# A rotary-embedding product moved from GpSimd to VectorE in a one-core attention and expert block

## The reference

```
q = x @ Wq.T + bq ; k = x @ Wk.T + bk ; v = x @ Wv.T + bv      # 16 heads of 64
def _rotate_half(x):
    half = x.shape[-1] // 2
    return concatenate([-x[..., half:], x[..., :half]], -1)
q = q * cos + _rotate_half(q) * sin
k = k * cos + _rotate_half(k) * sin
attn = softmax(einsum('bhqd,bhkd->bhqk', q, k) * scale)
out  = einsum('bhqk,bhkd->bhqd', attn, v)
x = layernorm(x + out @ Wo.T + bo)
x = layernorm(x + experts(x))
```

## Time and profile before

| | |
|---|---|
| median of 3 runs | 249.88 us (248.84 to 250.79) |
| the profiled execution | 248.74 us |
| its span, first to last instruction | 246.9 us |
| VectorE busy | 189.5 us (77%) |
| TensorE matmuls busy | 186.0 us (75%) |
| ScalarE busy | 157.4 us (64%) |
| GpSimd busy | 146.1 us (59%) |
| mean granted TensorE clock | 0.949 of full speed |

### The profile page before, as it was taken

The page is one execution under the profiler, slowest core; times in us unless marked ns, Lnnn a source line. Parts: engine busy times, 40 slices in busy tenths (PEclk is TensorE's granted clock), DMA queues, the critical chain, the costliest instruction groups (busy, mean ns, idle before and its releaser), DMA issues.

```text
span 246.9 us, 5191 instructions
## 1 busy us (share of the span) xinstructions
PE 186.0 (75%) x1817; PEld 129.4 (52%) x1817; DVE 189.5 (77%) x539; ACT 157.4 (64%) x321; POOL 146.1 (59%) x114
## 2 busy tenths in 40 slices
PE   1467799839768987876887897687685779998960
PEld 0121246626555765655566576455564655665660
DVE  6685747667978889888998887989989558359653
ACT  2558575928967976986997696795375374372300
POOL 6000084979989798797978879780480501000992
PEclk9999999968997997999999799999999799999996
DMA  7031224312122121221312213122100000000112
GB/s 248 40 77 31 62 69 123 85 25 65 37 52 64 47 66 38 54 58 43 75 36 54 66 39 75 33 57 54 32 3 5 0 4 0 0 3 0 44 45 85
DMA packets 12638, 12.30 MB, mean 50 GB/s; under 512 B 3116, under 2 KB 11716, under 8 KB 12612
## 3 DMA queue, kind: packets, MB, share of 16 engines
q1 hardware_dynamic: 12468, 11.70, 18.2%
q10 hardware_dynamic: 144, 0.26, 0.3%
HBM read 2.40 MB, written 1.05 MB: 14 GB/s over the span
## 4 chain that ended last, share of the span: by engine, by line
DVE 31%; POOL 25%; PE 25%; ACT 6%; DMA 5%; issue 5%; POOLq 0%; DVEq 0%
POOL by_cos L860 9%; DVE row_max L1018 9%; POOL by_sin L860 9%; DVE roped L982 7%; DMA qk<-mT_sb 5%; PE ps_t L422 4%; POOL y_sb L946 4%; ACT raw L716 3%; PE ps_m L466 3%; PE ps_m L361 3%; PE ps_s L378 3%; PE ps_s L388 3%; DVE o_sb L1041 3%; PE ps_o L439 2%; DVE hs L1244 2%
## 5 line engine op out<-in xcount | busy, mean ns | idle before, releaser
L735 ACT ACTIVATE probs<-ps_t 128x512 bf16<-128x512 f32 x128 | 77.2, 618 | 43.6 <-PE ps_t L422 43.0
L1018 DVE TENSOR_REDUCE row_max<-ps_s 128x2 bf16<-128x512 f32 x124 | 83.4, 675 | 21.2 <-PE ps_s L388 12.7
L860 POOL TENSOR_TENSOR by_cos<-raw,in_b 128x1024 bf16<-128x1024 bf16 x26 | 55.2, 2122 | 40.6 <-DVE roped L982 38.4
L716 ACT ACTIVATE raw<-ps_m,bqk 128x256 bf16<-128x256 f32 x128 | 53.6, 487 | 12.5 <-PE ps_m L361 8.5
L422 PE MATMUL ps_t<-qk 128*128 128x256 bf16 x256 | 53.5, 294 | 8.4 <-DMA qk<-mT_sb 8.4
L388 PE MATMUL ps_s<-qk 128*128 128x256 bf16 x224 | 45.8, 289 | 16.8 <-DVE row_max L1018 16.0
L860 POOL TENSOR_TENSOR by_sin<-raw,in_b 128x1024 bf16<-128x1024 bf16 x26 | 55.2, 2124 | 0.0
L439 PE MATMUL ps_o<-v_sb,probs 128*128 128x65 bf16 x512 | 38.6, 200 | 0.4 <-ACT probs L735 0.4
L361 PE MATMUL ps_m<-in_b 128*128 128x256 bf16 x128 | 30.0, 331 | 10.9 <-DMA in_b<-in_packed_b 4.2
L439 PEld LDWEIGHTS ps_o<-v_sb,probs 128*128 128x128 bf16 x512 | 34.0, 103 | 7.3 <-issue 1.1
L422 PEld LDWEIGHTS ps_t<-qk 128*128 128x128 bf16 x256 | 24.4, 103 | 17.3 <-DMA qk<-mT_sb 10.4
(11 more groups left out here) (127 smaller groups left out, 241.0 us busy)
## 6 DMA issues: line engine op xcount, KB each, us to landing
qk<-roped SPq DMA_DIRECT2D x128, 64.0 KB, 2.0
in_b<-in_packed_b SPq DMA_DIRECT2D x1, 770.0 KB, 6.5
out<-y_sb SPq DMA_DIRECT2D x3, 256.0 KB, 2.1
in_f<-in_packed_f SPq DMA_DIRECT2D x1, 586.0 KB
in_b<-in_packed_b SPq DMA_DIRECT2D x1, 512.0 KB, 4.5
in_b<-in_packed_b ACTq DMA_DIRECT2D x1, 256.0 KB, 3.6
qk<-mT_sb SPq DMA_DIRECT2D x16, 4.0 KB, 1.7
out<-y_sb SPq DMA_DIRECT2D x2, 128.0 KB, 1.8
```

What stands on the lines that cost most here:

```text
L716: last = nc.scalar.activation(raw[:, u % 2, g, a, half, :], ps_m[bank][:, half * S:half * S + S], ACT.Identity, bias=bqk[:, a, chunk:chunk ...
L735: nc.scalar.activation(probs[:, h % 4].rearrange("p c s -> p (c s)"), ps_t[h % 2][:], ACT.Exp, scale=DH ** -0.5).then_inc(exp_done, 1)
L860: last = nc.gpsimd.tensor_tensor(by[:, g].rearrange("p a h s -> p (a h) s"), raw[:, u % 2, g].rearrange("p a h s -> p (a h) s"), table[:]. ...
L1018: nc.vector.tensor_reduce(row_max[:, u % 2, h % 4, h // 4, :], of_head[:].rearrange("p (t s) -> p t s", s=S), AX_X, ALU.max, negate=True). ...
```

## The change

From unit 5 on (11 units, 5 to 15) GpSimd makes three products instead of four. The fourth, the sine product of the second group of heads, is made by VectorE, directly ahead of the rotation, with a semaphore `own_ready` between it and the rotation. `products_ready` is now signalled by GpSimd's third product. ScalarE's first copy into `raw` of a unit waits for `own_ready` of the unit two before, since VectorE now reads `raw` too.

```diff
+OWN_FIRST = 5
+        own_ready = sem("own_ready")
                 if g == 0 and a == 0 and u >= 5:
                     act.wait_ge(products_ready, u - 4)
+                    if u - 2 >= OWN_FIRST:
+                        act.wait_ge(own_ready, u - 2 - OWN_FIRST + 1)
                 last = nc.gpsimd.tensor_tensor(by[:, g].rearrange("p a h s -> p (a h) s"),
                                                raw[:, u % 2, g].rearrange("p a h s -> p (a h) s"),
                                                table[:].unsqueeze(1).broadcast_to([P, 4, S]), ALU.mult)
-                if piece == 3:
+                if piece == (3 if u < OWN_FIRST else 2):
                     last.then_inc(products_ready, 1)
                 if s["project"]:
-                    for piece in range(4):
+                    for piece in range(4 if T + 4 < OWN_FIRST else 3):
                         products(T + 4, piece)
                     else:
+                        if u >= OWN_FIRST:
+                            products(u, slice(1, 2), by_sin, sin_sb, own_ready)
+                            dve.wait_ge(own_ready, u - OWN_FIRST + 1)
                         dve.wait_ge(products_ready, u - 2)
                     if u >= 2:
                         dve.wait_ge(qk_in[(u - 2) % 4], copies_in(u - 2))
                     rotate(u, both, 0).then_inc(rope_ready, 1)
```

## The result

The changed kernel takes 257.3 us (median of 4 runs, 255.8 to 258.86), the kernel before, run beside it, 250.33 us. The ratio is 1.0283 with a 95% interval of 1.0198 to 1.0367: slower by 2.8%. The profiled execution took 257.62 us, its span is 255.8 us, 8.9 us longer than the profiled one of before.

What follows compares the result with a forecast made beforehand. Taken as bound: a VectorE-TensorE ring through each slot's rotation. Span 246.9 + 5.7 (+8.7 product, -3.0 waits) + 2.2 clock = 254.8 us, plus 1.84 around it = 256.6 us; range 252.3 to 259.6.

Steps and rivals of the forecast that it cites:

- What bounds the kernel: In every slot, a ring of VectorE and TensorE with the rotation as one link; VectorE busy 77% of the span.
- GpSimd's ring: Rotation, four products, next rotation: some 9.7 us, setting the time only where VectorE is early.
- The waits removed, 3.0 us: Rotations' waits for GpSimd's fourth product from unit 5 on all go, some 3.0 us in sum.
- The product, 0.79 us each: VectorE's added product and its wait ahead of the rotation in 11 units: 8.7 us, bounds 6.7 and 12.0.
- The row of unit 0: `by_sin` at 8.92, the rotation behind its semaphore at 9.71: 0.79 us from start to start.
- the rule of the Trainium skill: Chained VectorE instructions take the same time with a semaphore after each as at the end; the term would be 6.7 us.
- Sum without the clock, +5.7: Over the whole kernel: +8.7 us for VectorE's products less 3.0 us of waits for GpSimd.
- The clock, +2.2: TensorE's gap behind even units' rotations grows from 1.76 to 2.55 us; two more windows fall to 1.2 GHz, 2.2 us.
- the two alone that fell anew: The two windows behind even units' rotations that had kept full clock, expected to lose it: 0.80 + 1.44 us.
- the gap of 1.2 us that my rival named: Even slots: TensorE's gap comes near 1.2 us and the clock falls there too, five more falls, 261.6 us; chance 0.07.
- The clock stays as it is: TensorE's windows keep their clock: 254.4 us, chance 0.29; with a product of only 0.61 us 252.4, 0.05 more.
- VectorE's idle time takes the product in: VectorE's 12.7 us of waits ahead of row maxima absorb the product; 3.0 us gained, 245.7 us; chance 0.06.

Runs made afterwards that it cites:

- both gaps filled: Unread matmuls behind odd slots' rotations: 18 in the changed kernel (250.67 us, ratio 1.0089), 12 in the kernel before (246.53 us, 0.9906).
- the shift by one instruction: Changed kernel with 18 filling matmuls, VectorE's product moved ahead of the scaling of the third pair: 249.9 us, ratio 1.0043.
- the floor: Kernel before with GpSimd's fourth product made by nobody for units 5 to 15, plus 12 filling matmuls: 243.34 us, ratio 0.9772.
- the third experiment: Also called early: changed kernel with VectorE's product moved ahead of the slot's second row maximum, without filling: 249.63 us, ratio 1.0034.
- product added: Kernel before with GpSimd's four products kept, VectorE making the fourth once more into an unread tile: 257.52 us, ratio 1.032.
- left out: Kernel before with GpSimd's fourth product made by nobody for units 5 to 15, without filling: 246.07 us, ratio 0.9895.
- odd alone: Against the changed kernel, VectorE makes its product for odd units only, ahead of the second row maximum, without filling: 249.12 us, ratio 0.9991.
- changed again: The changed kernel unchanged, compared once more with the kernel before: 256.36 us, ratio 1.0281.
- the last run: Changed kernel with four unread matmuls in odd slots ahead of the scores that wait for the maxima row's copy: 255.71 us, ratio 1.0281.

## Why the prediction was right

It said 256.6 us; 257.3 and 256.36 were measured, and the mechanism is the one it gave. That the number came so near is in part luck. The growth of the profiled span, 8.9 us, is made up of 4.6 us with both gaps filled, 1.9 us of the clock's in the windows behind even units and some 2.5 us at slow copies. The forecast had 5.7, 2.2 and nothing: two terms too large and one missing. By the ratios of all runs the growth is less, 2.8% or 7.0 us, of which 4.6 stay with both gaps filled. Its steps:

*What bounds the kernel.* Right in the main. With GpSimd relieved or not, the product on VectorE costs about the same (257.52 against 257.3). GpSimd's ring is less of a side matter than it was made: with the clock held it is the limit in four of five windows.

*The waits removed, 3.0 us.* Right: 2.6 to 2.9 by themselves.

*The product, 0.79 us each.* The term was somewhat too large: 0.72. 0.61 of it is the product, 0.11 the wait, as the shift by one instruction showed. The row of unit 0 from which I took 0.79 has a rotation that waits for two semaphores; whether that is the difference wasn't tried. 11 x 0.72 = 7.9 instead of 8.7. By the rule of the Trainium skill that the prediction cites ("VectorE: DVE Perf Modes", The DRAIN you can't avoid) it would have been 0.61. Where a rotation waits for the product just ahead that does not hold; the choice against it was right.

*Sum without the clock, +5.7.* Shown as 4.6 with both gaps filled. There the waits removed are more than 3.0, since the kernel before meets GpSimd's ring in more slots once its clock holds: 7.9 - 4.6 = 3.3, and the floor's 3.2 says the same.

*The clock, +2.2.* The mechanism is right: the gap became 2.49 us for 2.55 forecast, all five windows fell, and filling the gap brought all five back. The total of what filling gives beyond the kernel before is 1.0281 - 1.0185, about 1.0% or 2.4 us. Its make-up is different from what I said. A fall costs 0.36 to 0.9 us rather than 0.80 to 1.44. Filling shortens the five windows behind even units by 3.6 us in the changed kernel and by 1.6 us in the kernel before, so 1.9 us of it are new. They come from all five windows, not from the two alone that fell anew. On top of that the profiled run lost some 2.5 us more than the kernel before at the slow copies of the maxima row, a term that the prediction does not have. The one fall behind an odd unit did not come by the gap of 1.2 us that my rival named (the gap behind that rotation was 0.48, in the other even slots 0.74 to 0.80), but behind the wait of 1.98 us for the copy.

*The rivals.* "The clock stays as it is" is out by the rows. "VectorE's idle time takes the product in" is out for this place: VectorE's waits for TensorE's scores didn't shrink (14.6 us in all, against 12.7). In the place of the third experiment it comes near to true. There the products are held up beside GpSimd's, of which none of my rivals spoke; that this alone makes the difference is not shown, since no run has the early product without the hold-up.

*Open:* the slow copies and the clock's share in the filling's gain. In the seven profiles without any filling (before, changed, product added, left out, early, odd alone, changed again) TensorE waits 1.2 to 2.0 us for the copy in slots 7 and 11; in all six with the gap filled it waits 0.8 us or less there, and up to 1.0 us in slot 8. The low clock does not make the copies slow: the last run has five low windows and a copy of 1.7 us in slot 11, and five of the six profiles at full clock have a slow copy in another slot. What goes with them is the load of instructions, as counted above. Why the loads fall on the copies so often, and that they delay them, no run shows. So the filling's gain is two things in these kernels: the clock held in the windows behind even units, and slow copies that came to stand where they cost less. The second hangs on where the loads of instructions fall, and need not come in another kernel.

## What to carry to other kernels

Before work is moved from an idle engine to a busier one, ask in which engine's program the next waiter stands: a product of 0.6 us in front of an instruction on which TensorE waits costs its length, its semaphore, and what the longer gap does to TensorE's clock. A short stretch of unread matmuls in such a gap can be worth more than the rearrangement (here 1% before, nearly 2% after the change, about half of it in windows with slow copies). Between VectorE and GpSimd, place an instruction with two SBUF inputs where the other engine is quiet.

## What the runs showed of the hardware that I had not expected

- A VectorE product started beside a GpSimd product, 0.17 us or more before its end, is held up and ends 0.54 to 0.56 us after the latter, in 26 cases in four profiles (0.72 to 1.53 us long instead of 0.68), while GpSimd's stays at 2.12 us.
- TensorE's clock fell in every one of the 20 windows behind a gap of 2.48 to 2.87 us (four profiles), and in all four behind 1.89 to 2.30 us. Behind gaps of 1.76 us it fell in 8 of 16 (before 2 of 4, left out 2 of 5, early 0 of 2, odd alone 4 of 5), so that gap leaves it open. In the 30 windows with a filled gap it never fell.
- A wait for the VectorE instruction just ahead costs 0.11 us; with another instruction between, nothing.
- Of 31 copies of the maxima row that took 2.3 to 3.0 us instead of 1.7, a 16 KB load of instructions started within 30, and within none of the 151 others.
